# Transformer decoder layer on one core: rotary halves exchanged by SBUF transfers, four of sixteen blocks by largest-eight and marking

## The chip, the cores and the metric

One core of one Trainium2 chip. The metric is the device time of one execution in microseconds (us). The kernel is one program with a stream of instructions for each engine: TensorE (PE, with its weight loads as PEld), VectorE (DVE), ScalarE (ACT), GpSimd (POOL) and SyncE (SP), which here only issues transfers.

## The reference

One decoder layer over x of shape (4, 256, 256), each of its three parts closed by a residual and a layer norm:

```
# 1. causal self-attention, 16 heads of 128, 2 key/value heads, no mask but the causal one
out = concat([x1*cos - x2*sin, x1*sin + x2*cos])     # rotary: x1, x2 are the lower and upper 64 of a head
logits = 30 * tanh(q @ k.T * 0.0884 / 30); causal; softmax; @ v; @ Wo
# 2. cross-attention, 16 heads of 16, query and output projections with rounded (8-bit) inputs and weights
# 3. feed-forward in 16 blocks of 64 hidden units, of which 4 are kept for each token
prob = softmax(xf @ Wr.T + br)                       # (tokens, 16)
_, idx = top_k(prob, 4); mask = 1 at idx, else 0
h = gelu(xf @ W1.T) * mask of its block;  y = h @ W2.T
```

Where two probabilities are equal, the lower index is kept.

## The kernel before

The four batches are cut into small operations in eight streams: `r` (the query and key projections with their rotation), `s` (scores), `m` (attention times values, turned and projected, and the first layer norm), `c` (context), `x` and `y` (cross-attention of the first and second 128 tokens), `n` and `o` (feed-forward of the first and second 128 tokens). The string `ORDER` (lines 135 to 141) has one letter for each of 533 operations and says from which stream the next one is taken. All engines walk the same list (`plan`) and issue their share of each operation, in that order and in no other. An engine whose next instruction has to wait holds everything behind it. SP does the same for transfers (lines 401 to 420): at `proj` it issues the load of a later piece of Wo (`load_wo`, line 362, 512 KB), at `wo` the store of a split piece (line 367), at `ffn` the store of the output.

PSUM is used as a ring of 7 banks; an operation takes the next one (two for some), and TensorE waits until the operation seven uses back has been read out.

The rotation. `rot` is operation i of nine in a batch: i = 0 makes both key heads, i = 1 to 8 a pair of query heads each. TensorE fills a bank [128 x 512] with 24 products (line 438, `three_pass`: each operand is split in a high and a low part). The partitions are the 128 dimensions of a head, so the two halves of the rotation are partitions 0 to 63 and 64 to 127. DVE's `rope` multiplies the bank by the cosines into `k_T` or `q_T` (line 928) and then makes the exchanged halves times the sines in `rope_t` (lines 931 and 932): reading partitions 64 to 127 and writing 0 to 63, and the other way. The sines are stored with opposite signs in the two halves. `rope_t` has two slots, taken in turn, and `rope` waits until the rotation two back has been added (line 916). POOL's `rotate` adds `rope_t` to the destination (line 1223). Then `near` and `far` (lines 469, 477) may use the heads. `near` for pair j needs rotation j + 1.

POOL's other work stands in the same order: the low part of the turned attention (`a_lo`, line 1234), the causal select on the probabilities (line 1241), the bias (line 1247) and the inverse roots of the layer norms (line 1252), for which DVE waits within the norm (line 958).

The router. `route` on DVE (`router`, lines 1107 to 1137) is run for eight tiles of 128 tokens. After the softmax over 16 blocks (lines 1114 to 1121) it compares all pairs: `above` is 1 where another block is larger (line 1125), `equal` where it is as large (line 1126), times `before_s` (line 1130), the sum of both (line 1132), the sum over the others (line 1134), and `keep` where that rank is under 3.5 (line 1137). Each of these but the last works on 256 elements a partition. `turn_m` turns `keep` on TensorE (line 653), ACT reads it out, and `hidden` spreads it over the hidden units (line 669) and multiplies the activations (line 1144).

Of the kernel before, what the change touches and what calls it, by code (L numbers as in the profile page):

```python
# [53 lines left out]
NBANK = 7  # L54
NEAR = 3
WO_SLOTS, WO_FLAT = 3, 3
CONSTS = 14
HPARTS = 2
PIECES = 5
PW = (NH + 2 * NKV) * HD // PIECES  # L60
# [62 lines left out]
def network_ops(b, t):  # L123
# [9 lines left out]


ORDER = (
    "rrrrrrrrrmmsrssrrmmsmrmssmrmmrrmmmsscmmmsmmmmmmccmmsssmmmcccmmmmrrmmmmccmmmrmmrrmsssmccmmmrmmsssmmmyrmmmx"
    "rsmssxyrmmmxmsmymrmmxsmysxxmmmmyrrymymmmxxxxysyryrmmrmyxyyxxxxyyxyxmmxyyxxymmmxmssxrrxyyxysxmymyyssxmmmmy"
    "xxccmmmsrsrnsmmmmsxyrcmcccmmymmsmsyxmrmmmxnmmmmmxxmnymrrnnyxxxxyyrxxxxmyxyyxxxxmyyxmmoxyyyxroyyxyymssxyym"
    "xosryyxroxysymysmmxmmsyccnoxymycomcomyccxsymnssrymxmymxxymyrxsxxmyxxyxxyyxyyyoymmxxyxxyxyymxyxxnyyxsxxsym"
    "yyxmmmmoxynmmmmmycmmcmmmmnxyccccooxnxyynxyxxyoyoxyyyyxyyxyyonxyyyxxxxyxxxyxyxxyyxxnyxyxyoxooyynnxnxnnnooo"  # L140
    "nnnoonoo")


def work_streams():
# [12 lines left out]
def make_plan():  # L157
# [13 lines left out]

PER_TILE = {"ln1": 5, "rstd1": 1, "ln2": 6, "ln3": 5, "rstd2": 1, "rstd3": 1, "y1_bias": 1, "quant_y": 6, "quant_o": 6, "y_T": 1,
            "query": 4, "q_T": 2 * QUADS, "xmasked": 4 * QUADS, "xexp": 4 * QUADS, "probs_T_even": QUADS,
            "probs_T_odd": QUADS, "xout": QUADS, "xattn": 2, "o_T": 1, "z_T": 1, "route": 10,
            "route_exp": 1, "mask_T": 1, "gelu": HPARTS, "masked": HPARTS, "stored": 16}


def build_decoder(nc, x, xT, ctxT, mask, wqkv, wo, wkvT, xwq, xwo, xbias, wrT, br, w1T, w2T,
# [10 lines left out]
    with ExitStack() as ctx:  # L189
# [24 lines left out]
        identb_s = sb("identb_s", [P], BF16)  # L214
        ones = sb("ones", [P])
        pick_s = sb("pick_s", [HT, P], BF16)
        before_s = sb("before_s", [NBLK, NBLK], BF16)
        half = sb("half", [TT])


        xT_s = sb("xT_s", [CK, T])
        x_hi, x_lo = sb("x_hi", [CK, T], F32R), sb("x_lo", [CK, T], F32R)
        rope_t = sb("rope_t", [2, 2, T])
        q_T = sb("q_T", [4, 2, T])
        k_T = sb("k_T", [NKV, T])
        v_s = sb("v_s", [TT, NKV, HD + 1])
# [27 lines left out]
        z_T = sb("z_T", [TT, CK, P])  # L254
        r_neg, r_sum, r_rec = sb("r_neg", [TT]), sb("r_sum", [TT]), sb("r_rec", [TT])
        r_in, prob = sb("r_in", [TT, NBLK]), sb("prob", [TT, NBLK])
        above = sb("above", [TT, NBLK, NBLK], BF16)
        equal = sb("equal", [TT, NBLK, NBLK], BF16)
        rank = sb("rank", [TT, NBLK])
        keep = sb("keep", [TT, P], BF16)  # L260
        keep_T = sb("keep_T", [T], BF16)

# [22 lines left out]
        wo_flat = [sem(f"wo_flat{i}") for i in range(WO_FLAT)]  # L285
        wo_out = [sem(f"wo_out{i}") for i in range(WO_SLOTS)]
        wo_hi, wo_lo = sem("wo_hi"), sem("wo_lo")
        piece_hi, piece_lo = sem("piece_hi"), sem("piece_lo")
        consts_set, bias_scaled = sem("consts_set"), sem("bias_scaled")
        quant_w, scale_diag, xw_T_done, xw_scale_done = (sem("quant_w"), sem("scale_diag"),  # L290
# [10 lines left out]

        def bank(kind, b, i=0, t=0, k=0):
            return banks[where[kind, b, i, t, k] % NBANK]

        def wait_filled(eng, kind, b, i=0, t=0, k=0):

# [29 lines left out]
        def _(sp):  # L336
# [27 lines left out]
            def store_wo(j):  # L364
# [2 lines left out]
                sp.dma_start(wo_parts[j], wo_s[:, j % WO_SLOTS].rearrange("p a m c -> p (a m c)").bitcast(F32))\  # L367
                    .then_inc(wo_out[j % WO_SLOTS], 16)

            def load_context(b):  # L370
                wait_filled(sp, "ctx", b - 1, 1)
                sp.dma_start(ctx_s[:], rows(ctxT[b])).then_inc(ctx_in, 16)
# [29 lines left out]
            for kind, b, i, t in plan:  # L402

                done.add((kind, b, i, t))
                both = all((kind, b, i, n) in done for n in range(TT))
                if kind == "quant_w" and i == 1:
                    load_tokens(1)
                elif kind == "wo":
                    store_wo(i)
                elif kind == "proj" and b * PAIRS + i + WO_SLOTS < B * PAIRS:  # L410
                    load_wo(*divmod(b * PAIRS + i + WO_SLOTS, PAIRS))
                elif kind == "outproj" and both and b + 2 < B:
                    load_tokens(b + 2)
                elif kind == "ctx" and i == TT - 1 and b + 1 < B:
                    load_context(b + 1)
                elif kind == "xscore" and i == QUADS - 1 and both and b + 1 < B:
                    load_mask(b + 1)
                elif kind == "ffn":
                    wait_for(sp, "ln3", b, 4, t)
                    sp.dma_start(out[b, t * P:(t + 1) * P, :], y3[:, t, :]).then_inc(sig["stored", t], 16)  # L420
# [4 lines left out]
        def _(pe):  # L425
# [223 lines left out]

            def turn_m(b, t):  # L650
                ps = claim("turn_m", b, 0, t)[:].bitcast(BF16)
                wait_for(pe, "route", b, 9, t)
                transpose(ps[:, 0:P], keep[:, t, :], identb_s[:]).then_inc(filled, 1)

            def hidden(b, part, t):
# [228 lines left out]
        def _(dve):  # L884
# [26 lines left out]
            def rope(b, i):  # L911

                ps = bank("rot", b, i)[:].rearrange("p (h q) -> p h q", h=2)
                n = b * (PAIRS + 1) + i
                if n >= 2:
                    dve.wait_ge(sig["rotated", 0], n - 1)
                if i == 0:
                    wait_filled(dve, "far", b - 1, QUADS - 1)
                    dst = k_T[:]
                else:  # L920
                    j = i - 1
                    wait_filled(dve, "far", *((b, (j - 4) // 2) if j >= 4 else (b - 1, (j + PAIRS - 4) // 2)))
                    dst = q_T[:, j % 4]
                wait_filled(dve, "rot", b, i)
                if b == 0:
                    dve.wait_ge(tables_in, 48)
                c, s = (a[:].unsqueeze(1).to_broadcast([P, 2, T]) for a in (cos_s, sin_s))
                v.tensor_tensor(dst, ps, c, ALU.mult).then_inc(sig["roped", 0], 1)
                lower, upper = slice(0, HD // 2), slice(HD // 2, HD)
                t = rope_t[:, n % 2]  # L930
                v.tensor_tensor(t[lower], ps[upper], s[upper], ALU.mult).then_inc(sig["roped", 0], 1)  # L931
                v.tensor_tensor(t[upper], ps[lower], s[lower], ALU.mult).then_inc(sig["roped", 0], 1)  # L932
# [174 lines left out]
            def router(b, t):  # L1107


                do, done = steps(sig["route", t], b * PER_TILE["route"])  # L1110
                wait_filled(dve, "route", b, 0, t)
                if b == 0:
                    dve.wait_ge(route_in, 32)
                do(v.tensor_tensor_reduce(out=r_in[:, t, :], in0=bank("route", b, 0, t)[:, 0:NBLK], in1=br_s[:], scale=-1.0,
                                          scalar=3.0e38, op0=ALU.add, op1=ALU.min, accum_out=r_neg[:, t:t + 1]))
                wait_for(dve, "route_exp", b, 0, t)
                do(v.tensor_reduce(r_sum[:, t:t + 1], prob[:, t, :], AX_X, ALU.add))
                done()
                do(v.reciprocal(r_rec[:, t:t + 1], r_sum[:, t:t + 1]))
                done()  # L1120
                do(v.tensor_scalar(prob[:, t, :], prob[:, t, :], r_rec[:, t:t + 1], None, ALU.mult))
                done()
                other = prob[:, t, :].unsqueeze(1).to_broadcast([P, NBLK, NBLK])
                own = prob[:, t, :].unsqueeze(2).to_broadcast([P, NBLK, NBLK])
                do(v.tensor_tensor(above[:, t], other, own, ALU.is_gt))
                do(v.tensor_tensor(equal[:, t], other, own, ALU.is_equal))
                done()
                if b == 0:
                    dve.wait_ge(consts_set, CONSTS)
                do(v.tensor_tensor(equal[:, t], equal[:, t], before_s[:], ALU.mult))  # L1130
                done()
                do(v.tensor_tensor(above[:, t], above[:, t], equal[:, t], ALU.add))
                done()
                do(v.tensor_reduce(rank[:, t, :], above[:, t], AX_X, ALU.add))
                done()
                wait_filled(dve, "turn_m", b - 1, 0, t)
                do(v.tensor_scalar(keep[:, t, 0:NBLK], rank[:, t, :], TOPK - 0.5, None, ALU.is_lt))

            def hidden(b, part, t):
                n = HT // HPARTS  # L1140
# [52 lines left out]
        def _(pool):  # L1193
            g = nc.gpsimd

            def constants():
# [8 lines left out]
                g.memset(xv_s[:, :, :, XD + 1:XW], 0.0).then_inc(consts_set, 1)  # L1205
                g.memset(identb_s[:], 1.0).then_inc(consts_set, 1)
                g.memset(pick_s[:], 1.0).then_inc(consts_set, 1)
                g.memset(before_s[:], 1.0).then_inc(consts_set, 1)
                g.memset(qS[:].bitcast(F32), 0.0).then_inc(consts_set, 1)
                g.memset(keep[:], 0.0).then_inc(consts_set, 1)  # L1210
                pool.wait_ge(consts_set, 10)
                select(identb_s[:], [[-1, P]], 0, 1, ALU.is_equal)
                select(before_s[:], [[1, NBLK], [-1, NBLK]], 0, 0, ALU.is_gt)
                select(pick_s[:], [[P, HT], [1, P]], 0, -BLK, ALU.is_ge)
                pool.wait_ge(consts_set, 13)
                select(pick_s[:], [[-P, HT], [-1, P]], BLK - 1, BLK, ALU.is_ge)

            def rotate(b, i):

                n = b * (PAIRS + 1) + i  # L1220
                dst = k_T[:] if i == 0 else q_T[:, (i - 1) % 4]
                wait_for(pool, "roped", b, 3 * i + 2)
                g.tensor_tensor(dst, dst, rope_t[:, n % 2], ALU.add).then_inc(sig["rotated", 0], 1)  # L1223

            def rest_wo(j):

# [89 lines left out]
```

## Time and profile before

| | us |
|---|---|
| median of 3 runs | 417.92 (417.89 to 418.08) |
| the profiled execution | 418.27 |
| its span | 416.5 |
| PE busy | 383.6 |
| DVE busy | 345.8 |
| ACT busy | 248.2 |
| POOL busy | 151.3 |

The profiled execution lasts 1.8 us longer than its span, which runs from the first to the last instruction. Busy shares are means over very different stretches: in the first 60 us weights arrive and are split, from there to about 330 us three or four batches overlap, and at the end only cross-attention and feed-forward of the last batch are left.

### The profile page before, as it was taken

Reading aid. Unit: us, or ns where it says so; the run is one execution under the profiler, and the core shown is the slowest. Engines: PE = TensorE matmul, PEld = TensorE weight load, DVE = VectorE, ACT = ScalarE, POOL = GpSimd, SP = SyncE. Lnnn points to the kernel's source line nnn. Section 1 sums busy time; section 2 is a strip of 40 time slices with the busy share of each in tenths; the row PEclk is TensorE's granted clock in tenths of the full one; section 3 lists DMA queues with packets and bytes.
Section 4 is the critical chain, followed back from the end, with each engine's and each line's share of the span. In section 5 each row is a group of like instructions: output and inputs, shape, how many; then the busy total and the mean of one; then the engine's idle time right before and its main releaser. Section 6 shows DMA issues by size and latency. Waiting matters only on the chain.

```text
span 416.5 us, 9192 instructions
## 1 busy us (share of the span) xinstructions
PE 383.6 (92%) x3144; PEld 327.9 (79%) x3144; DVE 345.8 (83%) x967; ACT 248.2 (60%) x528; POOL 151.3 (36%) x174
## 2 busy tenths in 40 slices
PE   2889999999999999999999999999889989889895
PEld 2868779887799877788998686978768977668784
DVE  4999987589989679889997998888798887888753
ACT  5266543545777775365689665389974247984230
POOL 7488636745544233455331133143113221000101
PEclk9999999999999999999999999999999999999999
DMA  6993342511311230213303000121103000000000
GB/s 213 334 344 127 124 144 89 182 48 51 102 50 53 84 121 2 76 58 105 121 1 102 2 27 27 39 65 51 52 27 103 2 0 14 15 2 0 14 15 25
DMA packets 16814, 31.36 MB, mean 75 GB/s; under 512 B 1665, under 2 KB 10753, under 8 KB 16769
## 3 DMA queue, kind: packets, MB, share of 16 engines
q1 hardware_dynamic: 15952, 29.98, 21.8%
q10 hardware_dynamic: 816, 0.79, 0.7%
q8 instruction: 27, 0.44, 0.4%
q14 instruction: 19, 0.15, 0.1%
HBM read 25.52 MB, written 5.24 MB: 74 GB/s over the span
## 4 chain that ended last, share of the span: by engine, by line
PE 48%; DVE 30%; issue 9%; ACT 6%; POOL 3%; DMA 3%; SPq 0%; DVEq 0%; POOLq 0%; ACTq 0%
PE bank L438 10%; PE acc L525 7%; PE bank L611 4%; PE bank L492 4%; PE bank L663 3%; PE bank L469 3%; PE bank L600 3%; ACT xs L817 2%; PE bank L506 2%; PE bank L623 2%; DMA xs<-in_wo 2%; PE bank L477 2%; DVE rope_t L932 2%; DVE rope_t L931 2%; PE bank L678 2%
## 5 line engine op out<-in xcount | busy, mean ns | idle before, releaser
L1223 POOL TENSOR_TENSOR q_T<-q_T,rope_t 128x512 f32<-128x512 f32 x32 | 43.0, 1345 | 45.0 <-DVE rope_t L932 45.0
L817 ACT ACTIVATE xs<-xs,xneg 128x256 f32<-128x256 f32 x128 | 54.5, 502 | 6.6 <-DVE xneg L1069 6.4
L1234 POOL TENSOR_TENSOR a_lo<-a_flat,a_hi 128x512 fp32r<-128x512 f32 x32 | 41.9, 1310 | 38.6 <-ACT a_flat L738 38.6
L438 PE MATMUL bank<-x_hi,wqkv_hi 128*128 128x256 f32 x144 | 45.6, 317 | 8.8 <-DVE wqkv_lo L904 8.8
L1252 POOL TENSOR_TENSOR rstd<-var_eps,half 128x1 f32<-128x1 f32 x24 | 13.2, 552 | 108.0 <-DVE var_eps L956 108.0
L525 PE MATMUL acc<-wo_s,a_hi 128*128 128x256 f32 x256 | 50.4, 295 | 0.9 <-POOL a_lo L1234 0.9
L1069 DVE CUSTOM_DVE_ANT_0 xs<-bank,mask_s 128x256 f32<-128x256 f32 x128 | 46.0, 418 | 0.6 <-PE bank L600 0.6
L492 PE MATMUL bank<-v_s,p_near 128*128 128x129 f32 x256 | 42.5, 278 | 1.2 <-POOL p_far L1241 0.8
L525 PEld LDWEIGHTS acc<-wo_s,a_hi 128*128 128x128 f32 x256 | 39.5, 189 | 3.8 <-issue 2.1
L492 PEld LDWEIGHTS bank<-v_s,p_near 128*128 128x128 f32 x256 | 35.8, 191 | 8.4 <-issue 6.6
L438 PE MATMUL bank<-x_lo,wqkv_hi 128*128 128x256 f32 x144 | 41.7, 289 | 0.0
L438 PE MATMUL bank<-x_hi,wqkv_lo 128*128 128x256 f32 x144 | 41.6, 289 | 0.0
L611 PE MATMUL bank<-ident_s,xs 128*128 128x128 f32 x256 | 36.2, 277 | 1.2 <-ACT xs L817 0.4
L438 PEld LDWEIGHTS bank<-x_hi,wqkv_hi 128*128 128x128 f32 x144 | 28.5, 198 | 10.5 <-issue 10.0
L525 PE MATMUL acc<-wo_s,a_lo 128*128 128x256 f32 x128 | 35.9, 280 | 0.0
L773 ACT ACTIVATE p_near<-bank 128x512 f32<-128x512 f32 x32 | 19.1, 596 | 26.7 <-PE bank L469 26.5
L738 ACT CAST a_hi<-bank 128x512 fp32r<-128x512 f32 x32 | 18.9, 591 | 24.3 <-PE bank L506 23.7
L611 PEld LDWEIGHTS bank<-ident_s,xs 128*128 128x128 f32 x256 | 28.4, 141 | 6.3 <-issue 3.4
L469 PE MATMUL bank<-q_T,k_T 128*128 128x512 f32 x64 | 32.3, 598 | 0.1
L663 PE MATMUL bank<-z_T,w_s 128*128 128x128 f32 x256 | 31.8, 277 | 0.5 <-DVE stage L1144 0.5
L663 PEld LDWEIGHTS bank<-z_T,w_s 128*128 128x128 f32 x256 | 30.0, 192 | 0.8 <-DVE stage L1144 0.7
L678 PE MATMUL bank<-w_s,stage 128*128 128x256 f32 x128 | 29.2, 381 | 0.5 <-DVE stage L1144 0.5
(150 smaller groups left out, 976.2 us busy)
## 6 DMA issues: line engine op xcount, KB each, us to landing
wo_s<-wo_parts SPq DMA_DIRECT2D x24, 512.0 KB, 3.3
wo_parts<-wo_s SPq DMA_DIRECT2D x8, 512.0 KB, 2.9
stage<-in_wqkv SPq DMA_DIRECT2D x5, 512.0 KB, 4.3
xs<-in_wo SPq DMA_DIRECT2D x8, 256.0 KB, 4.3
y<-in_x SPq DMA_DIRECT2D x4, 256.0 KB, 2.7
ctx_s<-in_ctxT SPq DMA_DIRECT2D x4, 256.0 KB, 4.7
mask_s<-in_mask SPq DMA_DIRECT2D x4, 256.0 KB, 2.7
w_s<-in_w1T SPq DMA_DIRECT2D x1, 1024.0 KB, 11.3
```

What stands on the lines that cost most here:

```text
L438: ins = mm(ps, lhs[i], rhs[j], start=(k == 0 and n == 0), stop=(last and n == 2))
L469: mm(ps[:, :], k_T[:, j // 4, 0:P], q_T[:, j % 4].rearrange("p h q -> p (h q)"), start=True, stop=True).then_inc(filled, 1)
L492: ins = mm(o, p_near[:, j % NEAR, m, t * P:(t + 1) * P], v_s[:, 0, j // 4, :], start=True, stop=(t == 0))
L525: ins = mm(acc[:, t, :], a[x], wo_s[:, slot, w, m, :], start=(j == 0 and t == 0 and m == 0 and p == 0), stop=(j == PAIRS - 1 and m == 1 an ...
L611: ins = transpose(ps[:, m2 * T + k * P:m2 * T + (k + 1) * P], xs[:, t, m, m2, k * P:(k + 1) * P], ident_s[:])
L663: ins = mm(ps[:, m * P:(m + 1) * P], w1_s[:, k, (n * part + m) * P:(n * part + m + 1) * P], z_T[:, t, k, :], start=(k == 0), stop=(k == CK ...
L678: ins = mm(ps[:, 0:C], g_T[:, t, n, :], w2_s[:, n, :], start=(n == 0), stop=(n == HT - 1))
L773: activation(dst, bank(kind, b, i)[:], ACT.Tanh, scale=SCALE / SOFTCAP).then_inc(sig["capped", 0], 1)
L817: activation(xs[:, t, m, m2, :], xs[:, t, m, m2, :], ACT.Exp, bias=xneg[:, t, m, m2:m2 + 1], scale=-1.0)\
L1069: do(v.tensor_tensor_reduce(out=xs[:, t, m, m2, :], in0=bank("xscore", b, g, t, m)[:, m2 * T:(m2 + 1) * T], in1=mask_s[:, t, :], scale=-1. ...
L1223: g.tensor_tensor(dst, dst, rope_t[:, n % 2], ALU.add).then_inc(sig["rotated", 0], 1)
L1234: g.tensor_tensor(a_lo[:, j % 2], a_flat[:, j % 2], a_hi[:, j % 2].bitcast(F32), ALU.subtract)\
```

## The change

Three things.

1. In batches 1 to 3 `rope` makes two products of full width instead of one full and two halves: first `rope_t` = bank times sines, without an exchange, then the product with the cosines. SP then issues two transfers within SBUF, 64 partitions by 2 KB each, which exchange the halves from `rope_t` into a new tensor `rope_s`. SP waits for the first product and for the rotation two back. POOL waits for both products and both transfers and adds `rope_s`. In batch 0 nothing changes.
2. The router finds the eight largest of the 16 probabilities (`max`), writes them behind four constants of -1, so that the first eight of the 12 values are these four and the four largest, and replaces each of these values where it occurs by -1 (`match_replace`); `keep` is where the result is negative. `before_s` and its two POOL instructions go; one small memset comes.
3. `ORDER` is another string of the same 533 letters, with each stream's own sequence unchanged.

```diff
-CONSTS = 14
+CONSTS = 13
 ORDER = (
-    "rrrrrrrrrmmsrssrrmmsmrmssmrmmrrmmmsscmmmsmmmmmmccmmsssmmmcccmmmmrrmmmmccmmmrmmrrmsssmccmmmrmmsssmmmyrmmmx"
-    "rsmssxyrmmmxmsmymrmmxsmysxxmmmmyrrymymmmxxxxysyryrmmrmyxyyxxxxyyxyxmmxyyxxymmmxmssxrrxyyxysxmymyyssxmmmmy"
-    "xxccmmmsrsrnsmmmmsxyrcmcccmmymmsmsyxmrmmmxnmmmmmxxmnymrrnnyxxxxyyrxxxxmyxyyxxxxmyyxmmoxyyyxroyyxyymssxyym"
-    "xosryyxroxysymysmmxmmsyccnoxymycomcomyccxsymnssrymxmymxxymyrxsxxmyxxyxxyyxyyyoymmxxyxxyxyymxyxxnyyxsxxsym"
-    "yyxmmmmoxynmmmmmycmmcmmmmnxyccccooxnxyynxyxxyoyoxyyyyxyyxyyonxyyyxxxxyxxxyxyxxyyxxnyxyxyoxooyynnxnxnnnooo"
-    "nnnoonoo")
+    "rrrrrrrmmrsrrssmmrrmsrmmssmrmmrsmmmmmmscsmmmmcsmmmrmcmmssmmrrcccmmmmmrrsmmmmmcmssmrrcmmmmmrmmmssmsmrrmccy"
+    "mssmmmmsxsmmmyxmmxssrmmmxymmmmmmmmxxmymmrrxyxmxxmmmyymsxyyxxxryrxxyyyxxxymyxyyxsxyyxyyyxxssrrymymmmxmyssc"
+    "scmmmxrssxccccrrmmyxmmxsnmmyxmmsxsxymmmxxmmmmxxryxnyrxxnnymmyymmmxxyyymryyxxxyyxyyyxryyroyxxoyymmyxmyxxcc"
+    "ssmmxossrrmmymxsmsmxccnmmmxysrccmoyxoymmyxmsxmnxxymxssxyooyxxxyxxyrxyymxxxnxyyyxxmyxyyymnxyyyyxmyyysyxosy"
+    "xymmmmmmyxmmmmynmmccmmmmnccccynoxoyoxyxnnyxyxoyxyxxoxyxynyxyyyxyxyyyxyxxyxyxxyyxxxoyxnoyxxynnxoyxnonynoon"
+    "onnoooon")
@@ SyncE
+            def swap_halves(b, i):
+                n = b * (PAIRS + 1) + i
+                lower, upper = slice(0, HD // 2), slice(HD // 2, HD)
+                if n >= 2:
+                    sp.wait_ge(sig["rotated", 0], n - 1)
+                wait_for(sp, "roped", b, 3 * i)
+                for dst, src in ((lower, upper), (upper, lower)):
+                    sp.dma_start(rope_s[dst, n % 2], rope_t[src, n % 2]).then_inc(swapped[n % 2], 16)
...
+                if kind == "rot" and b:
+                    swap_halves(b, i)
@@ VectorE, rope
+                if b:
+                    if n >= PAIRS + 3:
+                        dve.wait_ge(swapped[n % 2], 32 * swaps_before(n))
+                    v.tensor_tensor(rope_t[:, n % 2], ps, s, ALU.mult).then_inc(sig["roped", 0], 1)
+                    v.tensor_tensor(dst, ps, c, ALU.mult).then_inc(sig["roped", 0], 2)
+                    return
@@ VectorE, router
-                do(v.tensor_tensor(above[:, t], other, own, ALU.is_gt))
-                do(v.tensor_tensor(equal[:, t], other, own, ALU.is_equal))
+                do(v.max(best[:, t, 8 - TOPK:16 - TOPK], prob[:, t, :]))
                 done()
...
-                do(v.tensor_tensor(equal[:, t], equal[:, t], before_s[:], ALU.mult))
-                done()
-                do(v.tensor_tensor(above[:, t], above[:, t], equal[:, t], ALU.add))
-                done()
-                do(v.tensor_reduce(rank[:, t, :], above[:, t], AX_X, ALU.add))
+                do(v.match_replace(marked[:, t, :], best[:, t, 0:8], prob[:, t, :], -1.0))
                 done()
...
-                do(v.tensor_scalar(keep[:, t, 0:NBLK], rank[:, t, :], TOPK - 0.5, None, ALU.is_lt))
+                do(v.tensor_scalar(keep[:, t, 0:NBLK], marked[:, t, :], 0.0, None, ALU.is_lt))
@@ GpSimd
-                g.memset(before_s[:], 1.0).then_inc(consts_set, 1)
+                g.memset(best[:, :, 0:8 - TOPK], -1.0).then_inc(consts_set, 1)
...
-                select(before_s[:], [[1, NBLK], [-1, NBLK]], 0, 0, ALU.is_gt)
...
+                if b:
+                    pool.wait_ge(swapped[n % 2], 32 * (swaps_before(n) + 1))
+                g.tensor_tensor(dst, dst, (rope_s if b else rope_t)[:, n % 2], ALU.add).then_inc(sig["rotated", 0], 1)
```

## Rows read from the trace of the kernel before

**Rows 1.** The page, span and busy time of each engine.

```profile
span 416.5 us, 9192 instructions
PE 383.6 (92%) x3144; PEld 327.9 (79%) x3144; DVE 345.8 (83%) x967; ACT 248.2 (60%) x528; POOL 151.3 (36%) x174
```

**Rows 2.** Busy time by stretch; columns PE, PEld, DVE, ACT, POOL, clock, DMA, GB/s.

```profile
0.00:60.00 60.00, 49.08 (x307) 40.27 (x308) 51.03 (x89) 32.06 (x56) 40.02 (x49) 1.00 0.62 210
60.00:140.00 80.00, 78.36 (x645) 70.48 (x648) 66.55 (x160) 45.17 (x94) 43.28 (x44) 1.00 0.28 91
140.00:220.00 80.00, 77.22 (x646) 66.36 (x639) 69.74 (x200) 51.80 (x111) 31.87 (x34) 1.00 0.21 67
220.00:300.00 80.00, 77.17 (x676) 64.07 (x674) 69.00 (x225) 59.62 (x134) 20.54 (x27) 1.00 0.16 48
300.00:380.00 80.00, 72.33 (x677) 60.52 (x677) 68.25 (x233) 50.93 (x121) 12.32 (x15) 1.00 0.07 21
380.00:416.50 36.50, 29.40 (x205) 26.20 (x205) 21.26 (x65) 8.64 (x17) 3.30 (x6) 0.99 0.05 15
```

**Rows 3.** The page, the chain that ended last, by engine.

```profile
PE 48%; DVE 30%; issue 9%; ACT 6%; POOL 3%; DMA 3%; SPq 0%; DVEq 0%; POOLq 0%; ACTq 0%
```

**Rows 4.** Groups by line, the rotation: count, busy us, mean ns, idle before.

```profile
L928 DVE TENSOR_TENSOR q_T<-bank,cos_s 128x512 f32<-128x512 f32 x32 | 21.9, 686 | 5.1 <-PE bank L438 4.8
L931 DVE TENSOR_TENSOR rope_t<-bank,sin_s 64x512 f32<-64x512 f32 x36 | 25.0, 693 | 1.1
L932 DVE TENSOR_TENSOR rope_t<-bank,sin_s 64x512 f32<-64x512 f32 x36 | 24.6, 684 | 1.1
```

**Rows 5.** Chain in order of time (start, us, what): rotation products after 60 us.

```profile
102.05 0.13 DVE q_T L928
102.77 0.69 DVE rope_t L931
...
246.73 0.05 DVE rope_t L932
```

**Rows 6.** DVE in order of time (start, us): the last router.

```profile
398.44 0.42 DVE L1125 TENSOR_TENSOR above<-prob 128x256 bf16<-128x256 f32 x1
...
399.89 0.42 DVE L1134 TENSOR_REDUCE rank<-above 128x16 f32<-128x256 bf16 x1
400.34 0.17 DVE L1137 TENSOR_SCALAR keep<-rank 128x16 bf16<-128x16 f32 x1
```

**Rows 7.** Chain in order of time: two routers that stand on it.

```profile
307.59 0.42 DVE above L1125
...
362.11 0.42 DVE above L1125
```

**Rows 8.** PE in order of time, close to the end.

```profile
395.71 2.00 PE L663 MATMUL bank<-z_T,w_s 128*128 128x128 f32 x16
...
400.66 0.22 PE L653 MATMUL bank<-identb_s,keep 128*128 128x128 bf16 x1 [0.18 <-DVE keep L1137]
```

**Rows 9.** Transfers: count, KB each, median us from issue to landing.

```profile
wo_s<-wo_parts SPq DMA_DIRECT2D x24, 512.0 KB, 3.3
mask_s<-in_mask SPq DMA_DIRECT2D x4, 256.0 KB, 2.7
out_y<-stage SPq DMA_DIRECT2D x8, 128.0 KB, 1.7
```

**Rows 10.** One line, its issue time in ns (least, median, most).

```profile
L362 SPq DMA_DIRECT2D wo_s<-wo_parts x24: 319/319/374, 73.3 to 319.2; - x24
```

**Rows 11.** Chain in order of time: PE's share of some operations.

```profile
72.91 2.83 PE bank L438 x24
75.74 1.41 PE acc L525 x12
77.15 0.86 PE bank L469 x2
```

**Rows 12.** Chain in order of time: a rotation's add on POOL.

```profile
67.03 1.23 POOL k_T L1223
```

More of the change, by code:

```diff
@@ L135 @@
 ORDER = (
-    "rrrrrrrrrmmsrssrrmmsmrmssmrmmrrmmmsscmmmsmmmmmmccmmsssmmmcccmmmmrrmmmmccmmmrmmrrmsssmccmmmrmmsssmmmyrmmmx"
-    "rsmssxyrmmmxmsmymrmmxsmysxxmmmmyrrymymmmxxxxysyryrmmrmyxyyxxxxyyxyxmmxyyxxymmmxmssxrrxyyxysxmymyyssxmmmmy"
-    "xxccmmmsrsrnsmmmmsxyrcmcccmmymmsmsyxmrmmmxnmmmmmxxmnymrrnnyxxxxyyrxxxxmyxyyxxxxmyyxmmoxyyyxroyyxyymssxyym"
-    "xosryyxroxysymysmmxmmsyccnoxymycomcomyccxsymnssrymxmymxxymyrxsxxmyxxyxxyyxyyyoymmxxyxxyxyymxyxxnyyxsxxsym"
-    "yyxmmmmoxynmmmmmycmmcmmmmnxyccccooxnxyynxyxxyoyoxyyyyxyyxyyonxyyyxxxxyxxxyxyxxyyxxnyxyxyoxooyynnxnxnnnooo"
-    "nnnoonoo")
+    "rrrrrrrmmrsrrssmmrrmsrmmssrmmrsmmmmmmscsmmmmcsmmmrmcmmssmmrrcccmmmmmrrsmmmmmcmssmrrcmmmmmrmmmssmsmrrrmccy"
+    "mssmmmmsxsmmmyxmmxssrmmmxymmmmmmmmxxmymmrrxyxmxxmmmyymsxyyxxxryrxxyyyxxxymyxyyxsxyyxyyyxxssrrymymmmxmyssc"
[3 more added lines that the diff above has]
+    "onnoooon")
 def work_streams():
@@ L173 @@
             "query": 4, "q_T": 2 * QUADS, "xmasked": 4 * QUADS, "xexp": 4 * QUADS, "probs_T_even": QUADS,
-            "probs_T_odd": QUADS, "xout": QUADS, "xattn": 2, "o_T": 1, "z_T": 1, "route": 10,
+            "probs_T_odd": QUADS, "xout": QUADS, "xattn": 2, "o_T": 1, "z_T": 1, "route": 7,
             "route_exp": 1, "mask_T": 1, "gelu": HPARTS, "masked": HPARTS, "stored": 16}
@@ L216, in build_decoder @@
         pick_s = sb("pick_s", [HT, P], BF16)
-        before_s = sb("before_s", [NBLK, NBLK], BF16)
         half = sb("half", [TT])
@@ L222, in build_decoder @@
         x_hi, x_lo = sb("x_hi", [CK, T], F32R), sb("x_lo", [CK, T], F32R)
-        rope_t = sb("rope_t", [2, 2, T])
+        rope_t, rope_s = sb("rope_t", [2, 2, T]), sb("rope_s", [2, 2, T])
         q_T = sb("q_T", [4, 2, T])
@@ L256, in build_decoder @@
         r_in, prob = sb("r_in", [TT, NBLK]), sb("prob", [TT, NBLK])
-        above = sb("above", [TT, NBLK, NBLK], BF16)
-        equal = sb("equal", [TT, NBLK, NBLK], BF16)
-        rank = sb("rank", [TT, NBLK])
+        best, marked = sb("best", [TT, 16 - TOPK]), sb("marked", [TT, NBLK])
         keep = sb("keep", [TT, P], BF16)
@@ L287, in build_decoder @@
         wo_hi, wo_lo = sem("wo_hi"), sem("wo_lo")
+        swapped = [sem(f"swapped{i}") for i in range(2)]
         piece_hi, piece_lo = sem("piece_hi"), sem("piece_lo")
@@ L303, in bank, with swaps_before @@
             return banks[where[kind, b, i, t, k] % NBANK]
+        def swaps_before(n):
+            return len(range(PAIRS + 1 + (n - PAIRS - 1) % 2, n, 2))
         def wait_filled(eng, kind, b, i=0, t=0, k=0):
@@ L405, in _ @@
                 both = all((kind, b, i, n) in done for n in range(TT))
-                if kind == "quant_w" and i == 1:
+                if kind == "rot" and b:
+                    swap_halves(b, i)
+                elif kind == "quant_w" and i == 1:
                     load_tokens(1)
@@ L651, in turn_m @@
                 ps = claim("turn_m", b, 0, t)[:].bitcast(BF16)
-                wait_for(pe, "route", b, 9, t)
+                wait_for(pe, "route", b, 6, t)
                 transpose(ps[:, 0:P], keep[:, t, :], identb_s[:]).then_inc(filled, 1)
@@ L1122, in router @@
                 done()
-                other = prob[:, t, :].unsqueeze(1).to_broadcast([P, NBLK, NBLK])
-                own = prob[:, t, :].unsqueeze(2).to_broadcast([P, NBLK, NBLK])
-                do(v.tensor_tensor(above[:, t], other, own, ALU.is_gt))
-                do(v.tensor_tensor(equal[:, t], other, own, ALU.is_equal))
+                do(v.max(best[:, t, 8 - TOPK:16 - TOPK], prob[:, t, :]))
                 done()
@@ L1212, in constants @@
                 select(identb_s[:], [[-1, P]], 0, 1, ALU.is_equal)
-                select(before_s[:], [[1, NBLK], [-1, NBLK]], 0, 0, ALU.is_gt)
                 select(pick_s[:], [[P, HT], [1, P]], 0, -BLK, ALU.is_ge)
-                pool.wait_ge(consts_set, 13)
+                pool.wait_ge(consts_set, 12)
                 select(pick_s[:], [[-P, HT], [-1, P]], BLK - 1, BLK, ALU.is_ge)
@@ L1222, in rotate @@
                 wait_for(pool, "roped", b, 3 * i + 2)
-                g.tensor_tensor(dst, dst, rope_t[:, n % 2], ALU.add).then_inc(sig["rotated", 0], 1)
+                if b:
+                    pool.wait_ge(swapped[n % 2], 32 * (swaps_before(n) + 1))
+                g.tensor_tensor(dst, dst, (rope_s if b else rope_t)[:, n % 2], ALU.add).then_inc(sig["rotated", 0], 1)
             def rest_wo(j):
```

## The prediction

> **What bounds the kernel now.** I read the busy shares first [rows 1]: TensorE 383.6 of 416.5 us, DVE 345.8, the rest far behind. A mean hides the stages, so next came the table by stretch [rows 2]. From 60 to 300 us TensorE is busy 232.8 of 240 us; there it is the bound, and no faster DVE can give back more than the 7.2 us in which it idles. From 300 to 380 us it idles 7.7 us, and in the last 36.5 us it idles 7.1. In the first 60 us it idles 10.9 us, but there weights arrive and are split and batch 0 is rotated, which the change leaves alone. So in the whole stretch that the change touches and that is long enough to matter, 60 to 380 us, 14.9 us of TensorE idle stand against 320 us: that is the most that can be had outside of the tail, however much DVE work goes. The clock is at its full share in all of them and plays no part. The chain that ended last says who holds TensorE up [rows 3]: half of it is PE, 30% DVE, only 3% each POOL and transfers.
>
> The Trainium skill (Perfetto Trace Analysis, section "Identifying the Most-Contended Engine") holds matmul busy time to be a bad measure of how close TensorE is to its limit and takes the weight-load share instead, 79% here [rows 1]. By that rule more could be won than my sum has; this is the thought behind the "larger gain" rival below.
>
> **Part 1, the rotation.** Before, each costs DVE three products of 686, 693 and 684 ns [rows 4]: a half of 64 partitions costs as much as the full 128, because the time goes by the 512 elements. After, two products of full width, 2 x 686 = 1,372 ns. That removes 0.69 us from each of the 27 rotations of batches 1 to 3, 18.6 us of DVE. What of it lies on the path? On the chain after 60 us stand twelve pieces of rope_t, from 102.77 to 246.73 us, 7.0 us in all, and among them five of the cosine product, the first at 102.05, 2.8 us [rows 5]. A third of 9.8 us goes: **-3.3 us**.
>
> What it adds is a path by way of SP. Two issues at 0.32 us each [rows 10], and the landing. No transfer within SBUF is in this trace. The nearest row is the 128 KB store from SBUF, 1.7 us; the next, 256 KB, 2.7 us; and where a swap is queued behind a 512 KB piece of Wo, up to 3.3 us more [rows 9]. So the second half lands at least 1.7 + 0.3 = 2.0 us after the first product and at most 2.7 + 0.3 + 3.3 = 6.3 us. I take 2.0, since that row has the same size and leaves the same memory. One rotation then takes 0.69 + 0.1 + 2.0 + 1.3 (POOL's add, 1.23 on the chain [rows 12]) = 4.1 us from its first product to the end of the add, against 2.07 + 0.1 + 1.3 = 3.5 us before: 0.6 us later.
>
> Who waits for that? The scores. I gave each letter of the new ORDER its time on PE as the chain has it (2.83 us for a rotation's 24 products, 1.41 for a projection's 12, 0.43 for one score product [rows 11]) and summed: from the end of the products of a rotation in batches 1 to 3 to the first score product that needs it there are at least 6.6 us of other TensorE work (5.2 in the old string; the least is at the last rotation of batch 2, where two projections and one score product make half of it). That covers 4.1. The slot of rope_t comes round after two rotations, at least 8.7 us of TensorE work apart, so DVE does not wait at its new wait or the old one. Behind POOL's wait stand causal selects, a_lo and inverse roots. POOL is held about 2.0 - 0.7 = 1.3 us per rotation beyond the second product, 35 us over 27, and it has 265 us free [rows 1]. POOL is on the chain with a rotation in one place, from 67.03 us [rows 12], where Wo's last pieces are split; there and at one more place like it I let the delay through, 2 x 0.7: **+1.4 us**. In SP's queue a swap stands behind loads whose waits have been met by the time its own rotation is computed, since PE and DVE walk the same list. Only behind the stores of Wo in batch 0 can it be late, which is the place just counted. The 0.6 us of issuing per rotation lies on a queue that does little else.
>
> **Part 2, the router.** From the first comparison to the start of the last step it takes 400.34 - 398.44 = 1.90 us [rows 6]. After, `max` and `match_replace` on 16 elements. The nearest row is the 16-element comparison at 0.17 us, with 0.03 before it; from above, an instruction of 256 elements, 0.42 us. Two at least, 0.4 us; three of the long kind at most, 1.3 us. I take 0.4, as the work is 16 elements long: 1.5 us less in each of eight tiles (0.6 to 1.5), 12 us of DVE. The Trainium skill (VectorE: DVE Perf Modes, "Two Vector instructions with no wait between them") counts the match as two instructions, a load of the values and the replacement; by that it would be 0.6 instead of 0.4 us, and the total 0.4 us higher. On the path: the routers at 307.59 and 362.11 us are wholly on the chain [rows 7], 3.0 us. The last two are on the chain of DVE, but TensorE has `hidden` of the first tile meanwhile (from 395.71) and waits only 0.18 us for the second `keep` [rows 8], so they give 0.2. Sum **-3.2 us**.
>
> **Part 3, constants.** POOL loses a memset and a select and gains a small memset before the first rotation, which waits for products anyway: 0.
>
> **Part 4, the order and the slack.** DVE has 31 us less to do. Of the 14.9 us of idle, 6.5 are taken above; of the 8.4 left I give a third to the rest of the lighter DVE under an order made for it, between none and all: **-2.8 us**. This is the least founded term.
>
> **Sum.** -3.3 + 1.4 - 3.2 - 2.8 = -7.9 us. The profiled execution took 418.27 us (span 416.5 and 1.8 around it), so 410.4; the median of the runs shown lies 0.35 under it: **410.1 us**.
>
> **Rivals.**
> - *Larger gain.* The idle of TensorE from 60 to 380 us is nearly all DVE's doing, and products that run late behind one another hide more of it than busy time shows. For it: DVE is 83 to 87% busy in every stretch after 60 us [rows 2] and 30% of the chain. Against: neither order can take away every wait. All of the 14.9 us: 403 us. Chance 0.18.
> - *No change.* TensorE's own stream and ACT (60 of 80 us between 220 and 300 [rows 2]) take the place of DVE; what was won goes again in new waits. About 417.5 us. Against: two routers stand on the chain with nothing beside them. Chance 0.12.
> - *Slower, by late swaps.* One mechanism: the swap lands late, POOL stands at it, and the a_lo and causal selects behind it reach TensorE late. If it lands at 4.0 instead of 2.0 us, the 27 rotations, in some 16 groups of one or two, hold POOL 32 us longer; a third of that, POOL's busy share [rows 1], reaches the path: +11, 421 us. It decides from a landing of about 3.5 us. For it: each transfer touches 64 partitions only, each projection puts 512 KB on the same queue, and POOL is strictly in order. Against: 1.7 us for the same size [rows 9], and DMA only 7 to 28% busy after 60 us [rows 2]. Chance 0.15.
>
> The Trainium skill has a rule against such transfers (SBUF — State Buffer, "Can I just issue two DMAs to hit both halves?"): one over half of the partitions reaches half of the ports, and two over the two halves follow one another. No row here shows it. With its 196 GB/s and some 2 us fixed, my estimate from that page is 2 + 2 x 0.67 = 3.3 us of landing, just short of the point above.
>
> **Numbers.** Forecast 0.55 (roughly 406 to 415), larger gain 0.18, none 0.12, slower 0.15. The range 403 to 418 holds the first and third, and the second down to its price; it leaves out the slower case and a little below. A measurement of this kernel tells 0.2% (0.8 us) from no change. Faster takes the forecast, the larger gain and a third of "none": 0.77; within 0.2%: 0.06; slower 0.17.
>
> **What would show it.** DVE busy near 315 us; lines 931 and 932 down to the nine rotations of batch 0; the swap's landing near 2.0 us; POOL's idle before line 1223 larger, by transfers, without TensorE idle by POOL; the steps between 1121 and the last of the router at 0.4 us; TensorE's busy time unchanged and its idle between 60 and 380 us near 8 us. Wrong if the landing is over 3.5 us and waits of TensorE for a_lo or p_near grow, or if TensorE's idle moves elsewhere under the new order.

## The result and the profile after

The changed kernel takes 414.3 us (median of 5 runs, 413.0 to 415.5) against 417.9: a ratio of 0.992, 95% interval 0.989 to 0.994. It is faster, by 3.6 us where 7.8 were forecast. Its five runs scatter over 2.5 us; five runs of the kernel before over 0.7. The profiled execution took 413.8 us.

The page, span and busy times after:

```profile
span 412.1 us, 9281 instructions
PE 381.5 (93%) x3144; PEld 327.1 (79%) x3144; DVE 315.3 (77%) x924; ACT 246.8 (60%) x528; POOL 151.4 (37%) x173
```

DVE lost 30.5 us of work, as forecast (31). The span lost 4.4. The table by stretch, columns as in [rows 2]:

```profile
0.00:60.00 60.00, 47.73 (x314) 39.93 (x315) 49.58 (x85) 32.44 (x56) 40.03 (x49) 1.00 0.64 216
60.00:140.00 80.00, 79.19 (x607) 70.18 (x605) 53.92 (x149) 43.69 (x89) 43.45 (x44) 1.00 0.48 143
140.00:220.00 80.00, 76.28 (x687) 64.90 (x686) 65.94 (x199) 57.22 (x129) 29.28 (x32) 1.00 0.29 80
220.00:300.00 80.00, 78.52 (x697) 67.04 (x699) 64.71 (x212) 56.82 (x126) 24.18 (x29) 1.00 0.22 61
300.00:380.00 80.00, 73.47 (x677) 61.36 (x668) 64.45 (x226) 49.00 (x118) 11.16 (x14) 1.00 0.09 28
```

TensorE idles 12.5 us between 60 and 380 us, where I had expected 8 (14.9 before), and 1.4 us more than before in the first 60 (12.3 and 10.9). DVE is now idle a third of the time from 60 to 140 us, and TensorE is hardly busier for it than before.

The router and the transfers in the changed kernel: first the groups of DVE (mean ns), then the transfers with their median time to landing, then the issue times and landings of the same line:

```profile
L1143 DVE MAX8 best<-prob 128x8 f32<-128x16 f32 x8 | 1.4, 178 | 0.3
L1147 DVE MATCH_REPLACE8 marked<-best,prob 128x16 f32<-128x16 f32 x8 | 1.3, 159 | 0.0
L1147 DVE MATCH_VALUE_LOAD marked<-best,prob 128x8 f32 x8 | 0.7, 92 | 0.3
```

```profile
rope_s<-rope_t SPq DMA_DIRECT2D x54, 128.0 KB, 2.3
```

```profile
L380 SPq DMA_DIRECT2D rope_s<-rope_t x54: 461/548/1193, 59.6 to 289.4; - x54
...
DMA to landing us min/median/max: 2.2/2.3/4.2
```

Three instructions replace the comparisons, 0.48 us from the first to the last step (394.79 to 395.27 in the last router) where I took 0.4. The transfers are dearer than I took: an issue costs SP some 0.5 us instead of 0.32, and the landing is 2.3 instead of 1.7. In 14 of the 27 rotations POOL's add starts 3.04 to 3.12 us after the end of the first product, where I had 2.1; in the others it starts up to 5.0 us after it. The waits of POOL that the transfers end follow (total, times, longest). They hold the time before the product as well, in which POOL had nothing to do; in the kernel before, POOL's adds waited 52.4 us in all for DVE.

```profile
POOL q_T L1237 <- DMA rope_s<-rope_t: 54.4, 15, 9.4
POOL k_T L1237 <- DMA rope_s<-rope_t: 12.0, 3, 5.1
```

### The profile page after: what moved, and what is told of

Same layout as the page of the kernel before. It is cut to its first block, busy times and chain, and to the rows that moved or that the text cites. A ratio compares the mean times of both kernels' runs of the same rounds, so it can differ in the third digit from the quotient of the medians.

```text
span 412.1 us, 9281 instructions
## 1 busy us (share of the span) xinstructions
PE 381.5 (93%) x3144; PEld 327.1 (79%) x3144; DVE 315.3 (77%) x924; ACT 246.8 (60%) x528; POOL 151.4 (37%) x173
## 4 chain that ended last, share of the span: by engine, by line
PE 64%; DVE 17%; issue 7%; ACT 6%; POOL 3%; DMA 2%; SPq 0%; DVEq 0%; POOLq 0%; ACTq 0%
PE bank L452 12%; PE acc L539 8%; PE bank L625 6%; PE bank L692 5%; PE bank L677 5%; PE bank L483 5%; PE bank L506 4%; PE bank L614 3%; ACT xs L831 3%; PE bank L565 3%; PE bank L637 2%; PE bank L520 2%; PE bank L491 2%; PE bank L509 2%; DVE wqkv_lo L918 2%
## 5 line engine op out<-in xcount | busy, mean ns | idle before, releaser
L1237 POOL TENSOR_TENSOR q_T<-q_T,rope_s 128x512 f32<-128x512 f32 x24 | 31.1, 1301 | 54.7 <-DMA rope_s<-rope_t 54.4
L1266 POOL TENSOR_TENSOR rstd<-var_eps,half 128x1 f32<-128x1 f32 x24 | 13.2, 551 | 99.2 <-DVE var_eps L976 99.2
L506 PE MATMUL bank<-v_s,p_near 128*128 128x129 f32 x256 | 41.6, 277 | 1.5 <-POOL p_far L1255 1.1
L625 PE MATMUL bank<-ident_s,xs 128*128 128x128 f32 x256 | 37.7, 279 | 3.0 <-ACT xs L831 1.3
L1098 DVE COPY xp_T<-bank 128x512 f32<-128x512 f32 x32 | 21.9, 687 | 10.2 <-PE bank L625 10.0
L452 PEld LDWEIGHTS bank<-x_lo,wqkv_hi 128*128 128x128 f32 x144 | 28.0, 195 | 1.7 <-issue 1.7
```

Of the source, the lines that this page charges most:

```text
L452: ins = mm(ps, lhs[i], rhs[j], start=(k == 0 and n == 0), stop=(last and n == 2))
L506: ins = mm(o, p_near[:, j % NEAR, m, t * P:(t + 1) * P], v_s[:, 0, j // 4, :], start=True, stop=(t == 0))
L625: ins = transpose(ps[:, m2 * T + k * P:m2 * T + (k + 1) * P], xs[:, t, m, m2, k * P:(k + 1) * P], ident_s[:])
L1098: v.tensor_copy(xp_T[:, t, 1].rearrange("p m k q -> p (m k q)"), bank("turn_p", b, i, t)[:])\
L1237: g.tensor_tensor(dst, dst, (rope_s if b else rope_t)[:, n % 2], ALU.add).then_inc(sig["rotated", 0], 1)
```

## The experiments

Two factors were in the air: the latency of the transfers, and the order. Each ratio is taken against the kernel before in the same session (417.6 to 417.9 in all of them). Differences between two versions are differences of their medians, some of them across sessions. Where two traces are compared "start by start", TensorE's instructions are matched in order and the starts of the same instruction are subtracted.

**The parts alone and in pairs.** Each of these takes some of the three edits: the transfers with their full-width products ("exchange"), the router, the ORDER.

*Exchange left out of the changed kernel* (DVE's wait for the slot of `rope_t` goes with it).

```diff
-                if kind == "rot" and b:
-                    swap_halves(b, i)
...
-                if b:
-                    pool.wait_ge(swapped[n % 2], 32 * (swaps_before(n) + 1))
-                g.tensor_tensor(dst, dst, (rope_s if b else rope_t)[:, n % 2], ALU.add)
+                g.tensor_tensor(dst, dst, rope_t[:, n % 2], ALU.add)
```

> The changed kernel (414.3) without its 54 transfers: POOL adds rope_t itself, so the exchange of the halves, and with it the rotation's meaning, is left out in batches 1 to 3. Theory A (the transfers cost more than the 1.4 us that I let through: second half landed some 3 us after the product, POOL idle 66 us before its adds): 410 to 411 us. Theory B (the transfers are hidden, TensorE and the order are the bound): 413.5 to 414.5 us, within its scatter of the changed kernel.

Measured 410.4 us, and 411.0 when run again for its trace:

> The one without transfers again, for an undisturbed profile: 410.4 as before. Its trace against the changed kernel's should show in which stretch the 3.9 us are lost.

So the transfers with the wait for them cost 3.9 us (3.3 by the second session). Theory A.

*The new ORDER alone* (the one string exchanged in the kernel before).

> The kernel before (417.9) with nothing but the new ORDER. Theory A has no view of the order by itself, and takes it as neutral: 417 to 419. Theory B (the new order costs by itself, in the first 60 us above all, where TensorE idles 12.3 instead of 10.9 us, and is made for cheaper DVE work): 419 to 423 us.

431.1 us: 13.2 slower, worse than either theory had it. TensorE waits 5.9 us for `keep` alone, up to 2.3 us at a time:

```profile
PE bank L653 <- DVE keep L1137: 5.9, 3, 2.3
```

In the kernel before it was 0.18 us [rows 8]. The new string puts `turn_m` close behind `route`, and with a router that is 1.4 us longer this is costly.

*Router and new ORDER, three products as before.*

> New router and new ORDER, rotation as before on DVE (three products, no transfers). If the exchange by transfers is worth its DVE saving (my -3.3 + 1.4), this is slower than the changed kernel by 2 us or more, 416 or above. Theory A (the transfers cost as much as they save): 413 to 415. Theory B (DVE has slack under this order, so 18.6 us of DVE work hardly matter): 414 to 416.

420.5 us, as my terms had it (416 or above); both theories are out. Under this order DVE's rotation work is worth more than I had said: the exchange gains 6.2 us here with its latency, 10.1 without. Against the new ORDER alone (431.1) the new router gains 10.6 us. Start by start TensorE gets these 1.5, 0.3, 1.4, 0.8, 1.4, 1.4 and 1.4 us at the first seven of the eight routers, so nearly the whole of what is cut from most of them. The last 1.6 us come after the seventh, where with the old router TensorE waited and then ran for a while at the lower of its two clock levels (clock in the third column from the end):

```profile
406.00:411.00 5.00, 4.69 (x31) 4.62 (x32) 3.68 (x15) 1.92 (x4) 0.55 (x1) 0.71 0.08 28
```

*Exchange and new ORDER, old router.*

> Exchange by transfers and new ORDER, router as before. My term for the router was -3.2 us: then 417.4. If the order places the routers where nothing waits for them, 415 to 416; if more waits for them than I saw (TensorE waits 1.7 us for keep in the changed kernel), 419 or more.

428.5 us: 14 us more than the changed kernel. Not all of it is the router. In the traces (431.4 against 413.8 us) 3.6 us are lost between 82 and 97 us, and the first router stands at 206 us. So of the router's worth under the new order the 10.6 us above are the cleaner number, against 3.3 under the old one (below).

*Exchange alone, under the old ORDER.*

> The kernel before (417.9) with the exchange by transfers alone, old ORDER and old router. My terms for it: -3.3 + 1.4 = -1.9, so 416.0. Theory A (transfers late, POOL stands at them, and the old order leaves only 5.2 us to the first score product): 418 to 422. Theory B (hidden): 414.5 to 416.

429.8 us, 12 slower. My own forecast for this part, 416.0, missed by 14 us; theory A had the direction, and its range (418 to 422) ends 8 us short.

*The router alone.*

> The kernel before (417.9) with the new router alone. My term was -3.2 us, so 414.7. If the two routers on the chain have a near-critical path beside them, -1 to -2: 416 to 417.

414.6 us, ratio 0.993 (0.991 to 0.994): 3.1 to 3.3 us less, the term that I set, and the time of the whole change. Set start by start against the trace of before, TensorE gains 0.4 us at the first two routers, 0.7 by 304, 0.7 by 311, 0.7 by 366 and 0.9 in the tail. The routers at 307.59 and 362.11 us, which stood wholly on the chain [rows 7], thus gave 0.7 us each and not 1.5; the router at 298.6 us, which I had not counted, gave as much.

*Exchange and router under the old ORDER.*

> Both edits of the work under the old ORDER: the changed kernel less its order. My terms: -1.9 - 3.2 = -5.1, so 412.8, and then the new order made it slower. Theory B' (the edits are worth little and the new order is what makes them pay): 415.5 to 417.5.

425.9 us, 8.3 slower than the kernel before. B' fits in kind (the order makes the edits pay), not in size.

*The same without transfers*, that is old ORDER, new router, two full-width products, POOL adding rope_t:

> Old ORDER, new router, two full-width products and no transfers, POOL adds rope_t itself (the exchange is left out of the result). Against the new router alone (414.6) this is my term of -3.3 for the third product with nothing added: 411.3. If the term was right, 410.8 to 411.8, and the new order is worth only what is left to 410.4. If DVE was not what held this order up, 413 to 414.6, and the term itself was too large.

409.6 us. So the third product was worth 4.9 us under the old order (414.6 to 409.6), more than my 3.3, and the latency of the transfers costs 16.3 us there (409.6 to 425.9). Where the third product's gain comes in, start by start: in steps of 0.2 to 0.9 us at some nine places between 96 and 354 us. The new order without latency is not better than the old: 410.4, 0.7 us more, with intervals of the two ratios that overlap (0.981 to 0.983, 0.980 to 0.983).

**Latency or load?** The transfers stay, DVE still guards its slot, POOL does not wait:

```diff
-                if b:
-                    pool.wait_ge(swapped[n % 2], 32 * (swaps_before(n) + 1))
-                g.tensor_tensor(dst, dst, (rope_s if b else rope_t)[:, n % 2], ALU.add)
+                g.tensor_tensor(dst, dst, rope_t[:, n % 2], ALU.add)
```

> The changed kernel (414.3) with all its transfers issued and DVE still guarding the slot of rope_t, but POOL adds rope_t itself and waits for no transfer; the exchange is left out of the result. Theory A1 (the 3.9 us that the transfers cost are latency: POOL held at its wait and what stands behind it): 410.5 to 411.5, like the one without transfers. Theory A2 (they are load: SP's time to issue them ahead of the Wo pieces, and DMA traffic): 413.5 to 414.5.

410.4 us, the same as without any transfer. 7 MB more traffic and 54 more issues on SP cost nothing here; the whole 3.9 us come with POOL's wait and with what that wait shifts (the last section has one case).

**More latency.** The counts that DVE and POOL wait for are doubled with it.

```diff
                 for dst, src in ((lower, upper), (upper, lower)):
+                    sp.dma_start(rope_x[dst, n % 2], rope_t[src, n % 2]).then_inc(swapped[n % 2], 16)
+                for dst, src in ((lower, upper), (upper, lower)):
                     sp.dma_start(rope_s[dst, n % 2], rope_t[src, n % 2]).then_inc(swapped[n % 2], 16)
```

> The changed kernel with two more transfers of the same size ahead of each pair, into a scratch tensor, on the same semaphore: the exchanged halves come some 1.1 us later (two issues of 0.55). If latency reaches the path in a few places only, as 3.9 us for some 3 us of wait in 27 rotations says: +1 to +3, 415.5 to 417.5. If it is past a threshold, as under the old order (12 us): +6 or more.

428.6 us: 14.3 more. Run again for its trace:

> The one with two more transfers ahead of each pair, again, for an undisturbed profile: 428.5 us as before, and a granted clock under 0.99 in stretches where TensorE stood still, as in the exchange under the old order. The stretch that loses most should show POOL waiting for the transfers and TensorE for a_lo or the heads.

427.9 us, and both halves of the expectation hold. The mean granted clock is 0.993, but behind the wait at 78 us it fell:

```profile
80.00:85.00 5.00, 5.00 (x32) 4.68 (x31) 1.29 (x2) 4.94 (x10) 3.90 (x5) 0.73 0.49 165
```

The edit adds more than the 1.1 us that I had worked out. POOL's adds start 1.3 us later where a rotation stands alone (4.36 us after the first product, 3.07 before), but up to 3.9 us later where two follow one another, since four issues then stand before the second rotation's own on SP; the mean is 1.9. No run issues the four transfers without POOL's wait, so it is not shown that the load of four costs nothing, as that of two did. Of the 14 us, 8.8 are gone by 104 us (by the changed kernel's trace), in batch 1. TensorE's longest direct waits after the start, all three for POOL:

```profile
PE bank L485 <- POOL q_T L1239: 3.0, 2, 2.4
PE bank L508 <- POOL p_far L1257: 2.5, 2, 1.4
PE acc L541 <- POOL a_lo L1250: 2.0, 4, 1.0
```

A fourth goes by way of DVE, which waits for an inverse root on POOL within a norm and has a rotation's products behind it:

```profile
93.08 0.41 DVE L980 TENSOR_SCALAR y<-y,moments,rstd 128x256 f32<-128x256 f32 x1 [3.47 <-POOL rstd L1268]
95.69 0.69 DVE L947 TENSOR_TENSOR rope_t<-bank,sin_s 128x512 f32<-128x512 f32 x1
96.29 0.68 DVE L948 TENSOR_TENSOR q_T<-bank,cos_s 128x512 f32<-128x512 f32 x1
```

```profile
97.03 1.12 PE L493 MATMUL bank<-q_T,k_T 128*128 128x512 f32 x2 [1.53 <-DVE q_T L948]
```

At the same place 1.7 us are waited in the run with the exchange and the old router, and none in the changed kernel.

**Where it reaches the path.** Under the old order, the chain of "exchange and router" from 60 to 75 us (start, us, what):

```profile
65.45 1.30 POOL wo_s L1243
...
66.77 0.34 SPq L369
...
67.22 0.53 SPq L380
...
67.80 3.04 DMA rope_s<-rope_t
...
70.97 0.91 POOL k_T L1237
```

The swap of rotation 1.0 stands on SP behind the store of a split piece of Wo, which waits for POOL (`wo_s`, line 1243). POOL then comes to the rotation and waits for a transfer that could not be issued before. Its add starts 7.3 us after the first product. Before, POOL went straight on at 67.03 [rows 12]; here it starts at 70.97. Behind that add stands `a_lo`, and TensorE waits for it, and then runs at the lower level of its clock:

```profile
74.74 0.80 PE L539 MATMUL acc<-wo_s,a_hi 128*128 128x256 f32 x2 [4.21 <-POOL a_lo L1248]
```

```profile
75.00:80.00 5.00, 5.00 (x26) 5.00 (x27) 0.00 (x0) 1.26 (x3) 2.15 (x2) 0.55 0.65 215
```

Start by start against the same kernel without transfers, TensorE loses 4.3 us by the wait and 2.1 by the clock, 6.4 at one place. The new ORDER has rotations 1.0 and 1.1 ahead of that store: the first swap is issued at 59.6 us, before a store that waits until 69.1.

The second place under the old order costs 4.1 us by the same comparison: TensorE waits for the heads, and then again runs slower. TensorE in order of time, then the stretch itself:

```profile
106.02 1.23 PE L483 MATMUL bank<-q_T,k_T 128*128 128x512 f32 x2 [2.38 <-POOL q_T L1237]
107.05 1.91 PE L491 MATMUL bank<-q_T,k_T 128*128 128x512 f32 x2
108.75 0.63 PE L573 MATMUL bank<-identb_s,q_int 128*128 128x128 bf16 x4
```

```profile
105.00:110.00 5.00, 3.98 (x12) 2.22 (x13) 0.63 (x2) 2.14 (x4) 4.70 (x6) 0.69 0.53 157
```

From start to start the two products of line 491 take 1.70 us; two of the same size take 0.86 at full clock [rows 11]. After 2.4 us of idling TensorE is for a while at 1.2 instead of 2.4 GHz: 2.5 us are lost by the wait and 1.6 by the clock. The other 5 of the 15.5 us that the two traces differ by, from the first product on, are lost later, 2.2 of them near 193 us.

Under the new order, the chain of the changed kernel at rotation 2.0:

```profile
111.16 0.70 DVE rope_t L945
...
111.93 0.47 SPq L380
...
112.81 2.32 DMA rope_s<-rope_t
...
115.27 1.55 POOL k_T L1237
116.82 1.68 POOL a_lo L1248
...
118.55 0.50 PE acc L539 x2
```

Not the scores wait here: they need rotation 2.0 at 134 us. `a_lo` waits, the next item on POOL, and with it a projection on TensorE. Compared start by start with the trace in which POOL does not wait, TensorE loses 1.0 us here, 1.5 at 187, 0.5 at 257 and 0.5 in small steps before 90 us: with a last 0.1 at 206 us, 3.6 in all, as the spans differ (412.1 and 408.5).

**Taking places off the transfers.** Batch 1 back on DVE:

> The changed kernel with transfers in batches 2 and 3 alone; batch 1 makes three products as before. Nine rotations cost DVE 6.2 us more. Batch 1 is where the queues are fullest (DMA 48% from 60 to 140 us) and where the old order lost its 12 us. If the 3.9 us are lost there: 411 to 413, faster than both kernels. If DVE's time in batch 1 is worth more under this order than the latency: 415 to 418.

413.2 us, ratio 0.989 (0.988 to 0.991), and runs within 0.7 us of each other. That DVE's time in batch 1 is worth more than the latency (415 to 418) is out. The 1.1 us under the changed kernel are within the two intervals. Three rotations back on DVE:

> The changed kernel, with three of its 27 rotations back on DVE: 1.2, 2.0 and 2.8, behind whose adds TensorE lost 0.2, 0.9 and 1.5 us against the run in which POOL waited for no transfer. If these places carry the latency's cost: 414.3 - 2.6 = 411.7. If 0.69 us more of DVE in each, or the same loss at a neighbour, takes it back: 413.5 to 414.5.

415.3 us, from 412.7 to 417.4 over nine runs (ratio 0.991 to 0.996). The 411.7 of adding up the places is out; whether it is slower than the changed kernel is not told. In its trace (414.7) TensorE gets 0.8 us back at rotation 2.0 and none at 2.8, and loses 1.3 us at 92 us, where DVE's rotation products again stand behind a norm that waits for POOL (2.78 us, in the changed kernel 1.33). Batch 1 and two of these:

```diff
+        def by_transfer(n):
+            return n >= 2 * (PAIRS + 1) and n not in (18, 26)
...
-                if kind == "rot" and b:
+                if kind == "rot" and by_transfer(b * (PAIRS + 1) + i):
```

> As the one with transfers from batch 2 on (413.2), and rotations 2.0 and 2.8 on DVE as well. If the two places are independent of batch 1: 413.2 - 0.9 - 1.5 = 410.8, faster than both kernels; 413 or more if not.

412.7 us, ratio 0.989 (0.988 to 0.990), 1.9 short of what adding up the places gave. It has the lowest median of the versions that compute the reference, 1.6 us under the changed kernel's, but the intervals of the ratios overlap with that kernel's and with the one before it.

## Why the prediction was wrong, and what of it held

The forecast was 7.8 us less, the result 3.6. Two of its terms failed, the latency and the order; a third was too small and hid part of it.

**The router, -3.2: right in sum, not in place.** Measured 3.1 to 3.3 alone. But the two routers "wholly on the chain" gave 0.7 us each instead of 1.5, and routers that I had given nothing made up the rest. That the sum came out is luck: a step that stands wholly on the chain still has other work close beside it. My 0.4 us for the new steps was 0.48. The Trainium skill (VectorE: DVE Perf Modes, "Two Vector instructions with no wait between them") was right that the match is two instructions: 92 and 159 ns here.

**The third product, -3.3: under-sized.** It was worth 4.9 us under the order of which I read the chain, and 10.1 under the new one. The chain shows one path, and I took only what stood on it. That DVE work beside it held TensorE as well fits the many small steps in which the gain came, but is not shown place by place.

**The latency, +1.4: failed, it was 3.9.** Two numbers and one argument. The landing of 1.7 us came from a store to HBM of the same size, the issue of 0.32 from another shape; the path is 1.0 us longer (3.07 for 2.1). The Trainium skill's estimate in the prediction (SBUF — State Buffer, "Can I just issue two DMAs to hit both halves?"), 3.3 us for the landing of the pair, is nearer than my 2.0: measured, the second half lands some 2.9 us after the product. But two landings of 2.3 us each, issued 0.5 us apart, make that up, and no port limit is needed to explain it. The argument was worse than the numbers. I asked whether the scores wait, found 6.6 us of cover, and set POOL's hold against its idle time as a whole. The cover was real: in the changed kernel no score product waits for POOL. What is late is what stands behind the add on POOL, and what stands before the swap on SP. "A swap stands behind loads whose waits have been met" left out the stores of Wo, which wait for POOL itself; I let 0.7 us through there, and under the old order it is 6.4, a third of it by a clock that the prediction had said "plays no part".

**Order and slack, -2.8: failed, wrong in sign and meaning.** It was a third of the idle time that was left, a share with no row behind it. The new ORDER gives nothing by itself: 13.2 us slower on the old kernel, and no gain on the new work without latency. What it does is to make the latency cost 3.9 us instead of 16.3. Rotation and order together were forecast at -1.9 - 2.8 = -4.7 and gave -0.3 (414.6 to 414.3).

Term by term, along one path of runs: -3.3 router, -4.9 third product, +0.7 order, +3.9 latency = -3.6. This closes by construction, since each term is the step to the next run. Against the forecast it is 1.6 us better in the third product, 2.5 worse in the latency and 3.5 worse in the order. Along another path the same runs give +13.2 order, -10.6 router, -10.1 third product, +3.9 latency: what a term is worth depends on what stands beside it.

**The rivals.** "Slower, by late swaps" named the mechanism and the place behind it (a_lo on POOL) and put the point of decision at 3.5 us of landing. Under the old order that rival is what happened, with adds 3.0 to 3.1 us after the first product in 16 rotations and over 7 in three. Under the new one the adds had to come 1.3 to 3.9 us later than in the changed kernel for 428 us, so there is a steep rise beyond this change; where it begins is not shown. That it needs the order to stay below it, I had not seen. "No change, by TensorE's own stream" is out: without latency the same work takes 409.6.

What is left open: why the changed kernel and the one with three rotations back on DVE scatter so widely. The place near 90 us, where DVE waits for POOL and scores stand behind it, costs between 0 and 3.6 us in the traces of four runs, and may be part of it; one trace a run cannot show it. Not run either: the old order with the swaps issued ahead of the store of Wo, or from another engine's queue.

## What to carry to other kernels

A transfer put between two engines is a latency in two queues, not in one: list what stands before its issue and what stands behind its wait, on each in-order engine, and take no comfort from that engine's idle share. An order written for one set of durations belongs to them; when work and order change together, run the four combinations: here the work alone (425.9) and the order alone (431.1) were slower than the kernel before (417.9), and both together faster (414.3). And price latency by adding some: adds 1.3 to 3.9 us later cost 14.

## What the runs showed beside that

Two DVE operations with inputs in SBUF took about three times as long as usual while POOL was at work (medians of their lines: 0.43 us each). At 183 us in the changed kernel, on its path:

```profile
183.45 1.30 DVE L1070 TENSOR_TENSOR q_tmp<-q_tmp,bias_s 128x256 f32<-128x256 f32 x1
184.78 1.38 DVE L1075 CAST parts<-q_tmp 128x512 fp32r<-128x512 f32 x1
```

POOL at the same time:

```profile
183.20 1.27 POOL L1237 TENSOR_TENSOR q_T<-q_T,rope_s 128x512 f32<-128x512 f32 x1
184.43 1.45 POOL L1248 TENSOR_TENSOR a_lo<-a_flat,a_hi 128x512 fp32r<-128x512 f32 x1
```

In the run in which POOL does not wait for the transfers, its add comes earlier, and the same two take 0.80 and 0.43 us:

```profile
182.07 0.80 DVE L1070 TENSOR_TENSOR q_tmp<-q_tmp,bias_s 128x256 f32<-128x256 f32 x1
182.90 0.43 DVE L1075 CAST parts<-q_tmp 128x512 fp32r<-128x512 f32 x1
```

This is the 1.5 us at 187. So part of the latency's cost is no wait for a transfer at all: the add was moved onto another engine's work. The Trainium skill (SBUF — State Buffer, "Terms") has a port pair that DVE and GpSimd share, held for a whole instruction. The trace agrees: each of the two slow operations ends 0.3 us after an operation of POOL that was under way when it started.
